# Feed-forward part of layer 0: the first batch's normalisation, first two similarities and first half of the dense branch move into the rounds of the convolutions

## The reference, cut to what matters

```python
h = _layernorm(x) * (1 + ca) + sa
x = x + ga * attn0(h)            # projection, then 2 rounds: FFT convolution, product
h = _layernorm(x) * (1 + cb) + sb
x = x + gb * ffn0(h)

# ffn0(hidden):
q = einsum('btd,ed->bte', hidden, W_q)             # 2 halves x 4 heads x 64
sim = einsum('pbthn,hkpn->pbthk', q, keys)         # similarities to 2 x 64 keys for each head
scores_xy, idx_xy = top_k(sim, 8)                  # best 8 of each half
all_scores = sx[..., :, None] + sy[..., None, :]   # 64 sums
scores, pk = top_k(all_scores, 8)                  # best 8 pairs: the choice of keys
w = silu(einsum(hidden, down_embed[indices]) * softmax(scores))
experts = einsum(w, up_embed[indices])
dense = silu(hidden @ W_up.T) @ W_down.T           # inner width 512
return dense + experts
```

## Time and profile before

| | |
|---|---|
| median of 3 runs | 1162.44 us (1161.05 to 1164.18) |
| the profiled execution, its own time | 1161.96 us |
| its span, first to last instruction | 1160.7 us |
| PE busy | 1090.5 us, 94% |
| DVE busy | 937.8 us, 81% |
| ACT busy | 697.2 us, 60% |
| POOL busy | 421.2 us, 36% |
| granted TensorE clock, mean | 0.987 |

### The profile page before, as it was taken

One profiled execution on the slowest core, in us unless ns is written; L12 is line 12 of the kernel. 1 busy time (PEld: TensorE's weight loads), 2 busy tenths in 40 slices (PEclk: granted clock), 3 DMA queues, 4 the chain that ended last, 5 costly groups with the idle time before them and its releaser, 6 DMA issues.

```text
span 1160.7 us, 23183 instructions
## 1 busy us (share of the span) xinstructions
PE 1090.5 (94%) x7601; PEld 792.8 (68%) x7617; DVE 937.8 (81%) x3329; ACT 697.2 (60%) x1800; POOL 421.2 (36%) x707
## 2 busy tenths in 40 slices
PE   6798679999998999999999999999999999999997
PEld 5688446666666767777777777777776777656766
DVE  3988699999989599788888888888888898756767
ACT  1254345555566656777676767676767777745441
POOL 4400322233324135444444444444444555422310
PEclk9999889999999999999999999999999999999999
DMA  9200300000000000000000000000000000000000
GB/s 280 55 2 1 110 1 1 1 1 1 2 1 1 2 1 2 1 2 1 2 1 1 2 1 2 2 1 1 2 1 2 1 2 2 2 1 5 11 7 17
DMA packets 19957, 15.33 MB, mean 13 GB/s; under 512 B 2432, under 2 KB 18816, under 8 KB 19712
## 3 DMA queue, kind: packets, MB, share of 16 engines
q1 hardware_dynamic: 19840, 13.86, 4.1%
HBM read 12.81 MB, written 1.05 MB: 12 GB/s over the span
## 4 chain that ended last, share of the span: by engine, by line
PE 76%; DVE 13%; ACT 5%; issue 3%; POOL 1%; DMA 0%; SPq 0%; DVEq 0%; ACTq 0%; POOLq 0%
PE bank L1607 12%; PE bank L1637 11%; PE bank L1601 10%; PE bank L1556 8%; PE bank L1044 5%; PE bank L1945 5%; PE bank L1966 4%; PE bank L1577 3%; PE bank L1585 3%; PE bank L1029 3%; ACT prb L1672 2%; PE bank L639 2%; DVE prob L1362 1%; PE bank L1023 1%; PE bank L1004 1%
## 5 line engine op out<-in xcount | busy, mean ns | idle before, releaser
L1703 POOL TENSOR_SCALAR prb<-prb,rnorm 128x512 f32<-128x512 f32 (+3 forms) x512 | 270.4, 545 | 349.4 <-DVE rnorm L1793 349.3
L1672 ACT ACTIVATE prb<-prb,negmax 128x512 f32<-128x512 f32 (+3 forms) x512 | 280.9, 552 | 113.5 <-DVE negmax L1775 113.5
L1775 DVE CUSTOM_DVE_ANT_0 prb<-bank,mask 128x512 f32<-128x512 f32 (+3 forms) x512 | 218.7, 484 | 18.5 <-PE bank L1601 18.3
L1607 PE MATMUL bank<-ident,prb 128*128 128x128 f32 x1280 | 158.2, 275 | 3.4 <-POOL prb L1703 2.9
L1607 PEld LDWEIGHTS bank<-ident,prb 128*128 128x128 f32 x1280 | 139.6, 141 | 22.9 <-issue 12.0
L1637 PE MATMUL bank<-prbT,vv 128*64 128x512 f32 (+3 forms) x1024 | 152.0, 439 | 0.0
L1637 PEld LDWEIGHTS bank<-prbT,vv 128*64 128x64 f32 x1024 | 63.4, 137 | 82.4 <-issue 82.2
L1680 ACT ACTIVATE prbT<-bank 128x512 f32<-128x512 f32 x128 | 76.5, 598 | 62.0 <-PE bank L1607 60.1
L1784 DVE COPY prbT<-bank 128x512 f32<-128x512 f32 x128 | 87.8, 690 | 14.8 <-PE bank L1607 14.4
L1672 ACT ACTIVATION_READ_ACCUMULATOR prb<-prb,negmax 128x1 f32 x512 | 96.8, 189 | 0.0
L2003 ACT ACTIVATE h<-bank,eb1T 128x512 f32<-128x512 f32 x64 | 43.7, 687 | 53.8 <-PE bank L1945 53.6
(11 more groups left out here) (465 smaller groups left out, 2368.7 us busy)
## 6 DMA issues: line engine op xcount, KB each, us to landing
x<-in_x SPq DMA_DIRECT2D x2, 512.0 KB, 6.0
ew2T<-in_ew2T SPq DMA_DIRECT2D x1, 1024.0 KB, 7.7
ew<-in_ew SPq DMA_DIRECT2D x1, 1024.0 KB, 5.6
wq<-in_Wq SPq DMA_DIRECT2D x2, 512.0 KB, 5.1
wk<-in_Wk SPq DMA_DIRECT2D x2, 512.0 KB, 7.6
wv<-in_Wv SPq DMA_DIRECT2D x1, 1024.0 KB, 8.2
out<-res SPq DMA_DIRECT2D x16, 64.0 KB, 1.5
wmod<-in_wmod SPq DMA_DIRECT2D x2, 384.0 KB, 6.9
```

The costliest lines, as they stand in the source:

```text
L1607: last = T.transpose(into[:, at + (qc - kc) * P:at + (qc - kc + 1) * P], prb[j % 2][:, i, p_at[qc] + kc * P:p_at[qc] + (kc + 1) * P], iden ...
L1672: A.activation(v, v, ACT.Exp, scale=-1.0, bias=negmax[j % 2][:, place[qc], i:i + 1], accum_out=rowsum[j % 2][:, place[qc], i:i + 1]).then_ ...
L1703: last = G.tensor_scalar(v, v, rnorm[j % 2][:, place[qc], i:i + 1], 1.0, ALU.mult, ALU.mult)
L1775: V.tensor_tensor_reduce(prb[j % 2][:, i, p_at[qc]:p_at[qc] + (qc + 1) * P], s_of(j, s, i, qc), mask[:, (NT - 1 - qc) * P:S], 1.0, LARGEST ...
```

## The change: what it does

Four generators named `ahead` join the convolutions' rounds, one on each engine, behind the other streams in a round. Between them they hold: the statistics of batch 0 on VectorE (round 28), its normalisation on GpSimd (round 29), its transposes on TensorE (round 33), the scaling into `hT` (round 34, on ScalarE now and no longer on VectorE), the similarities of tiles 0 and 1 and the four dense quarters with their ScalarE parts (the following rounds). For these tiles banks 2 and 3 take the place of banks 4, 6 and 7. The four copies into `ew2R` and the one into `eb2R` go from VectorE to ScalarE. The choice of keys and everything behind it stay where they were, behind the convolutions. TensorE's wait for the copies moves to just ahead of the first `rank`. So that the new tiles can live beside the lanes, the overlay is laid out anew: `pre`, `hT`, `sim` and the others that are needed early lie at 2 * 4608 and up, and the two `gT` change places. A new semaphore `cv_done` counts finished batches of a lane.

```diff
@@ the end of the rotations, ScalarE
-            yield
+            yield from idle(6)
+            for j in range(E1 * HC // 4):
+                A.wait_ge(ew2_ps, j + 1)
+                A.activation(ew2R[:, 2 * j:2 * j + 2, :, :], bank[j % 2][:, :].rearrange("p (e c d) -> p e c d", e=2, c=HC), ACT.Copy).then_inc(ew2_kept, 1)
+                yield
+            A.wait_ge(ew2_ps, E1 * HC // 4 + 1)
+            A.activation(eb2R[:, :], bank[0][0:E1, 0:D], ACT.Copy).then_inc(ew2_kept, 1)
@@ the same, VectorE
-            for j in range(E1 * HC // 4):
-                yield
-                V.wait_ge(ew2_ps, j + 1)
-                V.tensor_copy(ew2R[:, 2 * j:2 * j + 2, :, :], bank[j % 2][:, :].rearrange("p (e c d) -> p e c d", e=2, c=HC)).then_inc(ew2_kept, 1)
-            yield
-            V.wait_ge(ew2_ps, E1 * HC // 4 + 1)
-            V.tensor_copy(eb2R[:, :], bank[0][0:E1, 0:D]).then_inc(ew2_kept, 1)
@@ the end of a batch in a lane, VectorE
-            dve.did(V.tensor_tensor(x[:, b, :, :], x[:, b, :, :], w.pv[:, :, 0, :], ALU.add))
-            dve.settle()
+            V.tensor_tensor(x[:, b, :, :], x[:, b, :, :], w.pv[:, :, 0, :], ALU.add).then_inc(w.cv_done, 1)
+            V.wait_ge(w.cv_done, n0 + 1)
@@ feed-forward, TensorE
+        AHEAD = bank[2:4]
-            T.wait_ge(ew2_kept, E1 * HC // 4 + 1)
-            turned(pre, 0)
-            sim(0)
-            for c in range(I_UP // P):
-                up(0, c)
-            sim(1)
-            logit(0, 0)
-            down(0)
+            def ahead():
+                yield from idle(32)
+                T.wait_ge(keys_ready, 1)
+                T.wait_ge(pre.ln_xhat, 1)
+                for t in range(NT):
+                    last = T.transpose(AHEAD[0][:, t * P:(t + 1) * P], pre.xhat[:, t, :], ident[:, :])
+                last.then_inc(pre.ln_ps, 1)
+                yield from idle(2)
+                T.wait_ge(layer0_in, LAYER0_IN)
+                T.wait_ge(pre.h_ready, 1)
+                sim_ahead(0)
+                up_ahead(0)
+                yield from idle(2)
+                T.wait_ge(ff_simk, 1)
+                sim_ahead(1)
+                T.wait_ge(ff_silu, 1)
+                up_ahead(1)
+                yield from idle(2)
+                T.wait_ge(ff_simk, 2)
+                up_ahead(2)
+                T.wait_ge(ff_silu, 2)
+                up_ahead(3)
+                yield
+            def main():
+                T.wait_ge(const_ready, 3)
+                T.wait_ge(ff_silu, NT)
+                T.wait_ge(lanes[0].cv_done, B // 2)
+                logit(0, 0)
+                down(0)
+                for n in range(TILES):
...
+                    if n == 0:
+                        T.wait_ge(ew2_kept, E1 * HC // 4 + 1)
+                    rank(n, 0)
@@ feed-forward, ScalarE
-            keep_sim(0)
-            for c in range(I_UP // P):
-                silu_up(0, c)
-            keep_sim(1)
-            exps(0)
+            def ahead():
+                yield from idle(33)
+                A.wait_ge(pre.ln_ps, 1)
+                A.activation(hT[0], AHEAD[0][:, :], ACT.Identity, bias=modT[0][:, 3, 0:1], scale=modT[0][:, 4, 0:1]).then_inc(pre.h_ready, 1)
+                yield from idle(2)
+                keep_sim(0)
+                silu_up(0, 0)
+                yield from idle(2)
+                keep_sim(1)
+                silu_up(0, 1)
+                yield from idle(2)
+                silu_up(0, 2)
+                silu_up(0, 3)
+                yield
+            def main():
+                exps(0)
+                A.wait_ge(const_ready, 3)
@@ feed-forward, GpSimd
-            normalised(pre, 0, 0)
-            past_of(0)
+            def ahead():
+                yield from idle(28)
+                normalised(pre, 0, 0)
+                yield
+            def main():
+                past_of(0)
@@ feed-forward, VectorE
-            statistics(pre, 0)
-            keep_before(0)
-            tops_of(0)
+            def ahead():
+                yield from idle(27)
+                V.wait_ge(const_ready, 3)
+                V.wait_ge(rows_kept, len(ROWS))
+                statistics(pre, 0)
+                yield
+            def main():
+                tops_of(0)
@@ TensorE's program; the other engines' read alike
             first_tensor()
-            together(batches(convolutions_tensor, 0), batches(convolutions_tensor, 1), setup_tensor(), rotations_tensor())
-            T.wait_ge(keys_ready, 1)
-            T.wait_ge(const_ready, 3)
-            T.wait_ge(layer0_in, LAYER0_IN)
-            last = feed_forward_tensor()
+            ff_ahead, ff_main, last = feed_forward_tensor()
+            together(batches(convolutions_tensor, 0), batches(convolutions_tensor, 1), setup_tensor(), rotations_tensor(), ff_ahead())
+            ff_main()
```

More of the change, by code:

```diff
@@ L1054, in experts @@
                 free["out"] = (ff_res, n + 1)
-            T.wait_ge(ew2_kept, E1 * HC // 4 + 1)
-            turned(pre, 0)
-            sim(0)
-            for c in range(I_UP // P):
-                up(0, c)
-            sim(1)
-            logit(0, 0)
-            down(0)
[L1064 to L1082, removed]
-                for b, c in up_at(n):
-                    up(b, c)
-                if n + 1 < TILES:
-                    logit(n + 1, 0)
-                    down(n + 1)
-                if n % 2 and n + 1 < TILES:
-                    sums(n - 1)
-                    dense(n - 1)
-                    experts(n - 1)
@@ new lines, in sim_ahead, with up_ahead @@
+            def sim_ahead(n):
+                T.matmul(AHEAD[1][:, :], tokens(n), msim[:, :, :, :].rearrange("p a h k -> p (a h k)"), start=True, stop=True).then_inc(ff_sim, 1)
+            def up_ahead(c):
+                T.matmul(AHEAD[c == 2][:, :], w_up[:, c * P:(c + 1) * P], hT[0], start=True, stop=True).then_inc(ff_up, 1)
+            def main():
[5 more added lines that the diff above has]
+                for n in range(TILES):
+                    before, after = normed_at(n)
+                    code(n)
+                    logit(n, 1)
+                    if n == 0:
+                        T.wait_ge(ew2_kept, E1 * HC // 4 + 1)
+                    rank(n, 0)
+                    rank(n, 1)
+                    if n + 2 < TILES:
+                        sim(n + 2)
+                    for h in (2, 3):
+                        logit(n, h)
+                        rank(n, h)
+                    if n % 2 == 0 and n:
+                        sums(n - 1)
+                        dense(n - 1)
+                        experts(n - 1)
+                    if n == 0:
+                        T.wait_ge(lanes[1].cv_done, B // 2)
+                    if before is not None:
+                        turned(pre, before)
+                    if after is not None:
+                        turned(post, after)
+                    for b, c in up_at(n):
+                        up(b, c)
+                    if n + 1 < TILES:
+                        logit(n + 1, 0)
+                        down(n + 1)
+                    if n % 2 and n + 1 < TILES:
+                        sums(n - 1)
+                        dense(n - 1)
+                        experts(n - 1)
@@ L1103, in last @@
                     experts(TILES - 1)
-            return last
+            return ahead, main, last
         def feed_forward_scalar():
@@ new lines, in ahead @@
+            def ahead():
[6 more added lines that the diff above has]
+                tops_of(0)
+                cast = best_of(0, *indices_of(0))
+                strike(0)
+                code_of(0, cast)
+                for n in range(TILES):
+                    before, after = normed_at(n)
+                    more = n + 1 < TILES
+                    if more:
+                        tops_of(n + 1)
+                    if before is not None:
+                        statistics(pre, before)
+                    if after is not None:
+                        V.wait_ge(ff_res, NT * after + NT)
+                        statistics(post, after)
+                    if more:
+                        at = indices_of(n + 1)
+                    if n >= 2:
+                        result(n - 2)
+                    gate_of(n, 0)
+                    if more:
+                        cast = best_of(n + 1, *at)
+                    gate_of(n, 1)
+                    if more:
+                        strike(n + 1)
+                    gate_of(n, 2)
+                    gate_of(n, 3)
+                    if more:
+                        code_of(n + 1, cast)
+                    if before is not None:
+                        keep_before(before)
+                    if after is not None:
+                        keep_after(after)
```

184 lines of the change are left out of this document (78 added, 106 removed).

## The result

The changed kernel took 1151.91 us (median of 4 runs, 1151.09 to 1152.45), the kernel before, run beside it, 1163.31 us (4 runs, 1161.05 to 1164.42). The ratio is 0.9906, with a 95% interval of 0.9892 to 0.9919. A second, later set of runs gave 1151.84 against 1162.15 us, ratio 0.9911 (0.9898 to 0.9925). The forecast was 1154.1 us, faster, range 1151.8 to 1157.6: the time lies in the range, 0.1 us above its lower end, with more gain than forecast.

The account below looks back on a forecast made before the run. TensorE was taken to bound the convolution stage's second batches, a serial chain with engines mostly idle the next 23 us. Terms -15.6 + 5.7 + 1.3 + 0.3 = -8.3 us gave 1154.1 us, range 1151.8 to 1157.6.

Parts of the forecast that it names:

- The bound of the stage: Second batches of the convolution stage: TensorE busy 33.27 of 33.50 us, so work put into its stream is paid in full.
- -15.6 for `tops_of`: End of the convolution stage: `tops_of` starts directly behind the last `x`, at 116.70 and not 132.29 us, 15.6 us saved.
- The three things that could hold `code`: Tile 0's `code`: TensorE's earlier work, ScalarE's copies, ScalarE's exponentials with table load; together cost nothing, up to 0.4 us.
- +5.7 on TensorE: Convolution stage: four transposes (+0.5) and six 512-column matmuls of 0.86 us (+5.2) lengthen TensorE's stream by 5.7 us.
- the slack of 0.2 us: Convolution stage, second batches: TensorE was taken to have only 0.2 us of slack in 33.5 for the added work.
- +1.3 for the statistics: VectorE, lane 1's first batch: statistics delay `x` and the squaring's update by 1.3 us, 1.2 if ScalarE had been last.
- +0.3 for the port: GpSimd's power and normalisations beside VectorE's L938 and L940, which read two SBUF tensors: 0.3 us lost, bounds 0 and 0.8.
- The first rival: GpSimd and VectorE lock each other out, L940 waiting out the whole power: 0.9 us more, 1155.0 us; chance 0.2.
- The low clock of tile 1: Rival, clock 0.50 from 154 to 160 us: without that stretch 1152.1 us (chance 0.08), with one more 1156.1 (0.07).
- No round slipped: Rival, new waits and a table load delay the convolution rounds: 1155.6 to 1157.1 us, chance 0.1, plus 0.05 for more.
- TensorE did not wait for GpSimd's rows: Rival, transposes ahead of both lanes and the rotations wait for GpSimd, kernel slower: time above 1166 us, chance 0.03.
- the forecast of -8.3: Whole kernel: sum of the terms, -15.6 + 5.7 + 1.3 + 0.3 us, expected to arrive at the end unchanged; chance 0.47.

## Why the prediction was right, and where it was off

**The bound of the stage** held: doubled matmuls cost 5.15 us for 5.16 of work, and there was no other room in the rounds.

**-15.6 for `tops_of`** is exact: 15.64 us became 0.04. `x` is followed by `tops` in the time that the earlier trace rows give for the same order, and the choice kept its 7.60 us. The three things that could hold `code` did not: TensorE was free 1.2 us early (forecast 1.3), `ebest` had 0.5 us to spare (forecast 0.4). The table load took 1.28 us and `ebest` started at 128.28, at once behind it: the second term that the Trainium skill (ScalarE: Activation LUTs, What ACT_TABLE_LOAD costs) puts behind a load did not show on the path here either.

**+5.7 on TensorE** was mis-sized: 4.96. The new instructions took what was forecast and 0.1 less: 85.37 - 84.93 = 0.44 us for the transposes, then 1.71, 1.72 and 1.72 for the pairs (89.79 to 91.50, 94.63 to 96.35, 99.47 to 101.19 us), 5.59 in all. But 0.63 us of delays of the kernel before are gone. This is its timeline there, of TensorE and of the VectorE instructions that it needed:

```profile
88.96 1.50 PE L639 MATMUL bank<-xm_e 128*128 128x128 f32 x12
...
90.09 0.42 DVE L914 TENSOR_TENSOR fold<-pv 128x256 f32<-128x256 f32 x1
...
90.56 1.86 PEld L857 LDWEIGHTS bank<-fold,c_fwd_sb 128*128 128x128 f32 x16 [0.30 <-DVE fold L914]
90.57 2.05 PE L857 MATMUL bank<-fold,c_fwd_sb 128*128 128x128 f32 x16
...
91.63 0.86 DVE L778 SCALAR_TENSOR_TENSOR xm_e<-bank,xm_over,xm_b 128x128 f32<-128x128 f32 x3
...
92.64 1.58 PE L639 MATMUL bank<-xm_e 128*128 128x128 f32 x12
...
94.05 1.95 PE L866 MATMUL bank<-spec_o,c_inv_sb 128*128 128x128 f32 x16
```

And the same instructions in the changed kernel, with new ones between:

```profile
91.50 1.50 PE L648 MATMUL bank<-xm_e 128*128 128x128 f32 x12
92.84 1.95 PE L859 MATMUL bank<-fold,c_fwd_sb 128*128 128x128 f32 x16
94.63 1.02 PE L1084 MATMUL bank<-msim,hT 128*128 128x512 f32 x2
...
96.35 1.50 PE L648 MATMUL bank<-xm_e 128*128 128x128 f32 x12
97.68 1.95 PE L868 MATMUL bank<-spec_o,c_inv_sb 128*128 128x128 f32 x16
```

From squaring to fold 1.61 us became 1.34, from fold to the next instruction 2.07 became 1.79, from squaring to inverse 1.41 became 1.33: 0.27 + 0.28 + 0.08. Before, TensorE reached operands that were just coming ready: L914 ended `fold` at 90.51 us and the transform started at 90.57, its weight load 0.30 us late for it, and L778 ended `xm_e` at 92.49 and the squaring started at 92.64. The new matmuls give these their time. The prediction counted only idle time (0.2 us) as slack, and part of this slack stood as longer busy time (2.05 against 1.95). Doubling the matmuls brought no second saving, as it should if the delays were already gone. What was mis-sized is thus the slack of 0.2 us that the prediction gave this stretch.

**+1.3 for the statistics** was 1.07. The first statistics start at 75.23 us and L940 at 76.48, so VectorE gives 1.25 us to them and not 1.32; and the squaring was let go 1.07 us later, its wait growing from 0.36 to 1.43. The prediction allowed 1.2 if ScalarE's xm_b had been the last before; but the squaring starts 0.14 us behind the end of VectorE's update in both kernels (78.42 and 78.56, 78.81 and 78.95), so the update decided before too. The timelines give the size: before, L938 starts 0.78 us behind the start of the instruction ahead of it (75.31 and 76.09), though that takes 0.68; in the changed kernel the statistics start 0.60 us behind it (74.63 and 75.23) and L940 another 1.25 later. 0.60 + 1.25 - 0.78 = 1.07. That L938 waits there because it reads the `pv` that the instruction before it writes, and the statistics do not, is inferred.

**+0.3 for the port** was 0 for VectorE. L940 and L942 took 0.69 us with and without GpSimd beside them; GpSimd's power paid 0.38 us, under its cover: `xhat_pre` ended at 81.3 us and TensorE's transposes came at 84.93. The first rival, 0.9 us more, is out, and the rule of the Trainium skill (SBUF — State Buffer, Who interferes with whom), by which the second to issue is blocked, fits only as far as GpSimd was the second to issue against L940 (76.66 against 76.48 us). L942 was issued at 77.21, within the power's 76.66 to 78.07, and took its 0.69 us all the same, which the rule does not give; times on GpSimd are rough in a profile, and no run here set out to let GpSimd go first.

**The other rivals.** The low clock of tile 1 stayed: from `code` to the first gate 148.70 - 143.85 = 4.85 us, before 4.84. No round slipped: all pairs stand at 0.86 us, with no idle time in front. TensorE did not wait for GpSimd's rows.

**The sum.** Term by term the forecast of -8.3 should have been +1.07 + 4.96 - 15.60 = -9.6. Nothing gave it back: from `code` on both kernels take the same within 0.3 us. The changed kernel's execution was also ahead by 0.7 us at the transpose, which is start-up. The forecast was thus short by 1.3 us in its terms (0.75 TensorE, 0.25 statistics, 0.3 port), and by 0.9 more through start-up and the rest behind `code`. That the time still lies in the range is in part luck: its lower end, 1151.8, stood for a lost low stretch at tile 1, and that stretch was not lost.

## What to carry to other kernels

Price work moved into a bound engine's stream at its full start-to-start time, but look for operands that come just in time there: instructions put between them can win back delays that hardly show as idle time. Look first at which engine makes the copies at a stage's end: moving five of them off the engine that starts the next chain gave 5.4 us alone. And fill the holes of a serial tail before the full rounds: the same four matmuls cost 3.4 us in the rounds and, by the trace, nothing in the tail.

## What the runs showed of the hardware

- Low clock stretches differ between executions of one kernel. One took 1155.8 to 1156.4 us in four runs and 1150.4 to 1150.9 us in two, with mean clocks of 0.985 and 0.989; in one execution the clock was at 0.51 from 28 to 35 us and in another at 1.00. The profiled execution of the copies alone has the clock low there too (0.57 from 28 to 36 us) and its transpose at 77.36 us. A single execution of such a kernel is good to some 5 us; marks inside the trace, counted from an instruction ahead of the change, agree to some hundredths (code at 55.77 and 55.80 us from the transpose in the two executions with the later statistics).
- Idle time ahead of the rotated weights does not settle their clock. Behind the same wait of 2.55 us they took 3.90 us with the copies alone on ScalarE, 5.47 us in the changed kernel and 6.68 us with the six matmuls behind them; and in the two executions of the kernel with the later statistics, 3.90 and 5.37 us. What decides it is open.
- GpSimd's power on 128x4 elements took 1.41 us beside VectorE's 0.69 us products and 1.03 us behind them, while VectorE's times did not change.
